# A Mamba scan beside a mixture of experts: who copies the last scan states, and when

## The reference

```python
xn = _layernorm(x, axis=-1)
x = x + _L0_attn_ref(xn, ...) + _L0_ffn_ref(xn, ...)
```

```python
def step(h, inp):
    u_t, d_t, b_t, c_t = inp
    dA = jnp.exp(d_t[..., None] * A)
    h = dA * h + (d_t * u_t)[..., None] * b_t[:, None, :]
    y = jnp.einsum('bdn,bn->bd', h, c_t)
    return (h, y)
```

## Time and profile before

| what | us |
|---|---|
| median of 3 runs | 912.57 (909.78 to 914.67) |
| the profiled execution, its own time | 911.35 |
| its span, first to last instruction | 909.3 |
| busy: VectorE / TensorE / GpSimd / ScalarE | 711.9 / 645.2 / 617.1 / 417.6 |

### The profile page before, as it was taken

One profiled execution on the slowest core, in us unless ns is written; L12 is line 12 of the kernel. 1 busy time (PEld: TensorE's weight loads), 2 busy tenths in 40 slices (PEclk: granted clock), 3 DMA queues, 4 the chain that ended last, 5 costly groups with the idle time before them and its releaser, 6 DMA issues. The chain is left out here.

```text
span 909.3 us, 15177 instructions
## 1 busy us (share of the span) xinstructions
PE 645.2 (71%) x4254; PEld 410.5 (45%) x4255; DVE 711.9 (78%) x889; ACT 417.6 (46%) x862; POOL 617.1 (68%) x388
## 2 busy tenths in 40 slices
PE   3630667615878787797787879779788878878871
PEld 2410355402555554454454545445545544545541
DVE  5889763631999999889989799899989988998210
ACT  1310333513556664564565456456546645644320
POOL 3727860001687888887887887788888878878642
PEclk9755568856999999998999799899989988979996
DMA  8644764992455365456446436635654654453332
GB/s 219 238 141 123 257 212 145 286 359 81 103 130 123 82 150 123 81 130 136 87 104 146 102 81 142 129 81 118 136 117 97 130 119 97 109 122 75 47 41 23
DMA packets 76699, 118.73 MB, mean 131 GB/s; under 512 B 22184, under 2 KB 56704, under 8 KB 74368
## 3 DMA queue, kind: packets, MB, share of 16 engines
q1 hardware_dynamic: 54656, 90.95, 36.5%
q0 software_dynamic: 19824, 27.16, 16.9%
q10 hardware_dynamic: 2192, 0.28, 0.4%
HBM read 83.00 MB, written 35.27 MB: 130 GB/s over the span
## 5 line engine op out<-in xcount | busy, mean ns | idle before, releaser
L546 POOL TENSOR_TENSOR ring<-ring,bc 128x1024 f32<-128x1024 f32 x128 | 316.5, 2487 | 43.3 <-DVE state L1073 41.0
L1069 DVE TENSOR_TENSOR_SCAN ring<-ring,state,pb 128x512 f32<-128x512 f32 x256 | 313.8, 1267 | 4.6
L1288 PE MATMUL py<-w2x,pool 128*128 x568 | 166.6, 446 | 5.6 <-ACT late L683 3.3
L665 ACT ACTIVATE ring<-late,aneg 128x512 f32<-128x512 f32 x256 | 163.8, 713 | 0.3
L1060 DVE TENSOR_TENSOR pb<-fb,bc 128x1024 f32<-128x1024 f32 x128 | 157.3, 1229 | 3.0
L519 POOL DMA_INDIRECT out_dram<-pool,meta x71 | 112.4, 1583 | 66.4 <-DMA out_dram<-late,idb 50.6
L1275 PE MATMUL fa<-w,pool 128*128 x284 | 143.9, 631 | 6.4 <-issue 5.3
L503 POOL DMA_INDIRECT pool<-xn_d,meta x71 | 71.5, 1008 | 110.1 <-DMA meta<-tab 81.7
L1288 PEld LDWEIGHTS py<-w2x,pool 128*128 128x128 f32 x568 | 121.6, 225 | 27.7 <-issue 8.7
L1275 PE MATMUL fb<-w,pool 128*128 x284 | 133.7, 593 | 0.0
L1261 PE MATMUL pt<-ident,pool 128*128 128x128 f32 x138 | 32.5, 322 | 141.5 <-DMA pool<-xn_d,meta 138.9
(11 more groups left out here) (214 smaller groups left out, 725.2 us busy)
## 6 DMA issues: line engine op xcount, KB each, us to landing
late<-dd_d SPq DMA_DIRECT2D x256, 128.0 KB
bc<-bc_d SPq DMA_DIRECT2D x72, 256.0 KB
w<-in_L_ffn_w_dram SPq DMA_DIRECT2D x16, 512.0 KB, 10.5
ring<-in_L_attn_x_dram SPq DMA_DIRECT2D x8, 512.0 KB, 4.4
xn_d<-w2x SPq DMA_DIRECT2D x8, 512.0 KB, 4.4
out_dram<-ring SPq DMA_DIRECT2D x8, 512.0 KB
dd_d<-pool SPq DMA_DIRECT2D x8, 512.0 KB, 3.6
w2x<-in_L_ffn_w_dram SPq DMA_DIRECT2D x8, 512.0 KB, 5.7
```

The lines of the kernel that those rows point to most:

```text
L546: ins = po.tensor_tensor(r, r, c_rows, ALU.mult)
L665: ins = ac.activation(ring[:, g % RING, n, :], dd[:, g % 2, 0, :], ACT.Exp, scale=aneg[:, NH * g + n:NH * g + n + 1])
L1069: ve.tensor_tensor_scan(r, r, pb[:, CH * m:CH * m + CH], state[:, NH * g + n:NH * g + n + 1], ALU.mult, ALU.add).then_inc(S["scan_done"], 1)
L1288: ins = pe.matmul(py[:, 0:D], ht[:, P * k:P * k + P], w2[:, bass.ds(e * (HC * D) + D * k, D)], start=(k == 0), stop=(k == HC - 1))
```

## The change

ScalarE, not VectorE, makes the copy into `state`. It is written as an activation Copy with the flag as scale. In iteration s of ScalarE's queue it stands behind `take_units` and ahead of `evac_xt`, and takes the states of unit s-1, so one iteration behind the scans. VectorE now waits for `h_ready` before it scans a group that starts from a copied state.

```diff
+            def keep_state(c, g):
+
+                ac.wait_ge(S["scan_done"], 4 * unit_index(c, g) + 4)
+                if not isinstance(c, int):
+                    apart(ac)
+                go_on = keep[:, c + 1:c + 2] if isinstance(c, int) else keep[:, bass.ds(c + 1, 1)]
+                ac.activation(state[:, NH * g:NH * g + NH], ring[:, g % RING, :, CH - 1], ACT.Copy, scale=go_on).then_inc(S["h_ready"], 1)
...
                     take_units(c, s)
+                    if s:
+                        keep_state(c, s - 1)
+                    elif not (isinstance(c, int) and c == 0):
+                        keep_state(c - 1, G - 1)
                     ac.wait_ge(S["b_done"], j)
...
                     take_units(NCH, j - REST[0])
+                if j == REST[0]:
+                    keep_state(NCH - 1, G - 1)
...
                     if half2 == 0:
                         ve.wait_ge(S["exp_done"], u + 1)
+                        if not (isinstance(c, int) and c == 0):
+                            ve.wait_ge(S["h_ready"], u - G + 1)
...
-                ve.wait_ge(S["scan_done"], 4 * u + 4)
-                go_on = keep[:, c + 1:c + 2] if isinstance(c, int) else keep[:, bass.ds(c + 1, 1)]
-                ve.tensor_scalar(state[:, NH * g:NH * g + NH], ring[:, g % RING, :, CH - 1], go_on, None,
-                                 ALU.mult).then_inc(S["h_ready"], 1)
```

## The result

The changed kernel takes 950.83 us (median of 4 runs, 946.85 to 957.9) against 912.47 us before (4 runs): ratio 1.043, 95% interval 1.0361 to 1.0499, slower. The profiled execution took 949.58 us, with a span of 947.8. Forecast were 947 and a range of 924 to 968.

The account below looks back on a forecast made before the run. The prediction took VectorE as the bound in chunk 0, GpSimd with its additions as or near the bound in chunks 1 to 7. Its terms gave 911.35 + 36 + 2 - 1 = 948, stated as 947, range 924 to 968.

Parts of the forecast that it names:

- GpSimd as the bound of chunks 1 to 7: Chunks 1 to 7: GpSimd with its additions is the bound or within 2.5 us a chunk of it.
- The price on ScalarE: ScalarE's copy: 0.25 us plus 0.15 to GpSimd's start, 0.4 in all; its 16 us of work lies in idle time.
- What is removed: VectorE loses 64 copies of 0.23 us, 14.7 us of work, some 0.3 us a unit with the gap.
- The move behind take_units: GpSimd's start waits for ScalarE's queue: later in 52 of 63 units, by 87.5 us in all, not the cost.
- The closed loop: Gather, TensorE, ScalarE's copy, GpSimd's start: two units per turn; 83.2 us a chunk, +36 over chunks 1 to 7.
- the ways back: From the end of GpSimd's gather to L700's end: 9.58 us at high clock, mean 10.6, plus 0.4 for the copy.
- The mixed path: GpSimd's units 3, 4, 6, 7, 1 with three returns through ScalarE: 82.0 us a chunk at high clock, 83.2 taken.
- Chunk 0: VectorE is the bound there; 8.95 us a unit against 9.04, so a change of 0 to -1 us.
- The last unit: Its copy waits for L700 of the first iteration behind the loop: +2 us.
- (1): Rival: GpSimd's delay is absorbed as heavy units shorten, only +2 is left, 913 us; chance 9%.
- (2): Rival: VectorE sets the pace, 0.3 us less for each unit, 19 us faster, 892 us; chance 5%.
- (3): Rival: TensorE's clock falls behind longer waits, +13 us a chunk in chunks 1 to 7, 1003 us; chance 9%.

Follow-up runs that it names:

- Run 7: Kernel before, but GpSimd itself copies the states ahead of its multiplies, waiting only for the scans; 929.88 us, ratio 1.0176.
- run 8: Kernel before with GpSimd's next gather moved ahead of the expert's addition; 881.32 us, ratio 0.9651.
- run 9: Changed kernel with GpSimd's next gather moved ahead of the expert's addition; 886.05 us, ratio 0.9694.
- run 2: Kernel before plus a same-size ScalarE copy of constants at the new copy's place, for which nobody waits; 910.15 us, ratio 0.9972.
- run 1: Kernel before, VectorE still copying, with GpSimd waiting in addition for ScalarE's take of the sum of the unit before; 949.71 us, ratio 1.0453.
- run 3: Changed kernel with ScalarE's copy two steps earlier in its queue, between put_du and evac_ht; 914.05 us, ratio 1.0034 to the kernel before.
- run 4: Changed kernel with ScalarE's copy between evac_ht and take_units; 928.79 us, ratio 1.0168 to the kernel before.
- run 6: Changed kernel with two 8x512 constant copies on ScalarE directly ahead of the copy of the states; 988.47 us, ratio 1.0842 to the kernel before.
- run 10: Kernel before with both ScalarE's copy behind put_du and the gather ahead of the expert's addition; 879.96 us, ratio 0.9665.

## Why the prediction was right

**GpSimd as the bound of chunks 1 to 7.** Right. Run 7 added some 0.4 us a unit there and lost 16 us; runs 8 and 9 took waiting out of it and won 32 us on the kernel before and 67 on the changed one.

**The price on ScalarE.** The copy takes 0.31 us (300 to 314 ns) where I took 0.25, and GpSimd starts 0.39 behind L700's end where I took 0.4, since the copy overlaps L700. That its work is covered is shown by run 2. The reason given for the cover was read too generously: in the example of the rows L700 was not long done when TensorE turned the rows at 472.28, it had ended at 472.15. What covers the copy is that ScalarE was idle for 0.60 us between that L700 and L719.

**What is removed.** Taken too small: 64 times the median is 14.7 us, but with the stretched ones the 64 copies took 19.3 us. VectorE's busy time fell by 21.5. It changed nothing, since VectorE isn't last.

**The move behind take_units.** Right, and the only cause: run 1 has it without the move of the copy, runs 3 and 4 take it back in two steps.

**The closed loop.** The sum had 83.2 us a chunk; measured are 571.92 / 55 x 8 = 83.2, +35.3 us for +36 forecast. Its parts held as well: the ways back have a mean of 10.6, as read before, and the three that the mixed path uses have 10.2, 10.1 and 10.0, with 0.4 each for the copy, where 10.4, 10.1 and 10.0 with 0.4 each were read (the table under run 6 has the landings as they really were, which makes the third 10.3). The mixed path can be followed in the starts of the multiply: unit 3.3 at 502.65, 3.4 at 514.30 right behind it, 3.6 at 535.70, 3.7 at 546.53, 4.1 at 567.46, 4.3 at 586.93, together 84.3. That the exact figure was hit is luck, because I chose it between 82.0 and 84.0, and because the misses of chunk 0 and of the last unit, below, nearly cancel: the forecast was 36 + 2 - 1 = +37 on the profiled execution, and +38.2 was measured. Run 6 shows that this loop gets stiffer when more is put on the way, since more units then wait for the copy, so three ways a chunk is a lower estimate.

**Chunk 0.** Wrong in sign, small: +2.05 us for 0 to -1. The six ways that I read there (0.2 to 0.7) have a mean of 10.2 us instead of 9.7, one of them 11.3 with a slow down and up (2.85 and 2.71 us where 1.9 is usual); the granted clock of the stretch is 0.95, and was 0.98. I had left the clock out of this term. I had also left out the way of unit 0.1, which took 11.1 us before and 11.2 after. VectorE's gain of 0.27 us a unit is real: runs 3, 7 and 10 show it in chunk 0, where the way doesn't cover it.

**The last unit.** +2 was forecast for it and did not come. Unit 7.7 starts at 880.76, 0.02 us behind the end of its gather, and its copy had been done at 879.99: GpSimd was late by itself there, as in most second units of a heavy pair.

**Rivals.** (1), absorbed: the landing waits stayed at 41.5 us (41.3 before), nothing gave way. (2), VectorE's relief decides: only in chunk 0 and only with a place that leaves GpSimd alone. (3), the clock: granted 0.92 in chunks 1 to 7 both times; there it fell only when the way was made 1 us longer (0.89). In chunk 0 it fell from 0.98 to 0.95, see above.

## What to carry to other kernels

When work moves to an idle engine, ask at which place of that engine's queue it lands and who waits for it: here 64 copies of 0.3 us cost nothing as work and 38 us as a place. If the waiting engine issues a transfer behind its wait, the delay comes back as a closed loop; add up one turn of it with rows of the profile, and count the turns. An engine at 83% busy can be the bound when much of the rest is waits for landings (41.3 of 91.6 us here); putting an independent issue into such a wait won more (3.5%) than the moved copy could have (19 us, 2.1%, had VectorE set the pace).

## What the runs showed of the hardware

A copy of 128x4 takes 0.23 us on VectorE, 0.31 on ScalarE with a scale from memory, and 0.20 on GpSimd. In run 1 VectorE's copy had 258 ns in the median and up to 3605. Every copy of over 1 us on VectorE (3 in the kernel before, 11 in run 1) lay beside a multiply of GpSimd and ended 0.03 to 0.04 us behind that multiply's end, as if held by it; the longest, 768.79 to 772.40, had begun 0.6 us before the multiply of 769.41 to 772.36. GpSimd starts 0.08 to 0.09 us behind the end of ScalarE's copy in the unrolled chunk 0, and mostly 0.18 to 0.19 in the loop. There the value waited for comes from a register and one more instruction (`apart`) stands behind the wait; which of the two costs the 0.1 us was not separated. Copies that follow each other on ScalarE overlap: 128x256 took 0.42 us and delayed the next by 0.30. In the changed kernel TensorE was already waiting for gathered rows in 51 of the 52 ways of chunks 1 to 7, and took them up 1.7 to 2.0 us after the gather's issue ended in 45 of them; the others took up to 2.9. In the kernel before it was 30 of 46, the others up to 4.0.
